# ODE layer inside the eigenvector block: matrix scaled ahead of V's scaling and the row statistics, powers copied at shorter distance

## What is computed

```
h = jnp.einsum('bnd,ed->bne', x, fc_in_w) + fc_in_b
alph = jax.nn.sigmoid(alpha_train)[:, None]
w_eff = w * jnp.clip(d, 0.0, 1.0) @ w.T
for _ in range(8):
    ax = jnp.einsum('nm,bmd->bnd', adj_mx, h)
    h = h + (1/8) * (alph * 0.5 * (ax - h) + h @ w_eff - h + x0)
```

## Time and profile before

| | us |
|---|---|
| median of 3 runs | 6786.41 (6783.37 to 6788.06) |
| profiled execution, device time | 6792.14 |
| its span, first to last instruction | 6790.4 |
| busy in the span: PE, DVE, ACT | 5355.4, 4564.6, 2311.9 |
| the block of the change, about | 4084 to 4673 |
| V's scaling in it | 4093.00 |
| recurrence in it | 4116 to 4551 |
| loop over batches on PE in it | 4192.09 to 4596.4 |

### The profile page before, as it was taken

How to read it: one execution, slowest core, us unless ns; L and a number is a source line. 1 busy time by engine, 2 the same in 40 slices (tenths; PEclk the granted TensorE clock), 3 DMA queues, 4 the chain that set the end, 5 groups by cost and what they waited for, 6 DMA issues and landing times. The chain is left out here.

```text
span 6790.4 us, 109815 instructions
## 1 busy us (share of the span) xinstructions
PE 5355.4 (79%) x33047; PEld 3803.4 (56%) x33047; DVE 4564.6 (67%) x27007; ACT 2311.9 (34%) x7369; POOL 93.6 (1%) x128
## 2 busy tenths in 40 slices
PE   4666788888877769969899976993546699776999
PEld 4555566666666534446566653662333477554676
DVE  7888888888888853379999997775562333424333
ACT  1222222222222235449599881110110233201333
POOL 0000000000000000000000000000000000000000
PEclk9999999999999999969999987996778799876999
DMA  1000000000000000010000000000000000000000
GB/s 46 2 2 2 2 3 5 3 4 4 4 4 3 4 21 13 7 54 6 6 4 6 4 3 8 1 1 0 25 28 0 13 0 0 9 0 13 0 0 25
DMA packets 27823, 56.57 MB, mean 8 GB/s; under 512 B 6186, under 2 KB 16835, under 8 KB 25539
## 3 DMA queue, kind: packets, MB, share of 16 engines
q1 hardware_dynamic: 27330, 50.79, 2.2%
HBM read 38.20 MB, written 12.58 MB: 7 GB/s over the span
## 5 line engine op out<-in xcount | busy, mean ns | idle before, releaser
L2007 DVE SCALAR_TENSOR_TENSOR f_ACC<-f_yp,f_CG,f_ACC 128x128 f32<-128x128 f32 x1024 | 288.4, 344 | 461.6 <-DVEq L2005 461.6
L1952 PEld LDWEIGHTS f_yp<-f_W,f_hs 128*128 128x128 f32 x4096 | 490.0, 192 | 92.6 <-issue 91.8
L1886 PE MATMUL f_hp<-f_rows,f_W 128*128 128x512 f32 x1024 | 531.5, 602 | 5.1 <-ACT U L1896 3.0
L1054 ACT ACTIVATE e_XD<-e_X,e_scal 128x60 f32<-128x60 f32 x2048 | 527.5, 333 | 17.5 <-DVEq L918 15.7
L710 PE MATMUL h_small<-h_part,ones 128*128 128x2 f32 x1024 | 300.6, 363 | 294.3 <-DVE h_jd L579 198.4
L1983 ACT ACTIVATE f_hs<-f_hp,f_b 128x512 f32<-128x512 f32 x512 | 347.7, 685 | 539.7 <-ACTq L1982 539.7
L655 ACT ACTIVATE h_VW<-h_v,h_s 128x8 f32<-128x8 f32 (+3 forms) x512 | 154.8, 302 | 1082.6 <-DVE h_s L417 1082.6
L1942 PE MATMUL f_hp<-f_XT,f_W 128*128 x1024 | 484.4, 601 | 33.0 <-PEq L2236 33.0
L703 PEld LDWEIGHTS h_ax<-h_XM,h_parts 128*128 128x128 bf16 x11520 | 480.8, 114 | 40.9 <-issue 40.9
L1952 PE MATMUL f_yp<-f_W,f_hs 128*128 128x128 f32 x4096 | 493.5, 275 | 0.0
L710 PEld LDWEIGHTS h_small<-h_part,ones 128*128 128x128 f32 x1024 | 256.6, 311 | 415.0 <-DVE h_jd L579 287.6
(11 more groups left out here) (716 smaller groups left out, 11363.2 us busy)
## 6 DMA issues: line engine op xcount, KB each, us to landing
f_S<-in_f_W SPq DMA_DIRECT2D x64, 128.0 KB, 2.3
X<-in_x SPq DMA_DIRECT2D x1, 4096.0 KB, 16.3
held<-g0e_HL SPq DMA_DIRECT2D x16, 256.0 KB, 2.0
g_HL<-held SPq DMA_DIRECT2D x16, 256.0 KB, 2.8
f_W<-in_f_W SPq DMA_DIRECT2D x2, 2048.0 KB
spill<-f_xts SPq DMA_DIRECT2D x16, 256.0 KB, 2.0
f_rows<-spill SPq DMA_DIRECT2D x16, 256.0 KB, 2.7
f_W<-in_f_W SPq DMA_DIRECT2D x4, 1024.0 KB
```

The lines of the kernel that those rows point to most:

```text
L1054: ins = nc.scalar.activation(XD[b][:, k, h, :], X[:, :], ACT.Identity, bias=scal[b][:, k, 2 * h:2 * h + 1])
L1886: nc.tensor.matmul(self.hp[s % 3][:, :], self.W1[:, e, j * P:(j + 1) * P], self.rows[:, g % 2, :], start=True, stop=True).then_inc(self.h_ ...
L1952: ins = nc.tensor.matmul(yp[:, u % 2, k, :], hs[:, u % 2, c, k * P:(k + 1) * P], W2[:, u * UC + c, :], start=(c == 0), stop=(c == UC - 1))
L2007: ins = V_.scalar_tensor_tensor(ACC[:, k, :], yp[:, u % 2, k, :], CG[:, k * E + e:k * E + e + 1], ACC[:, k, :], ALU.mult, ALU.add)
```

## The change

`start` loses the `bn_stats` and the row statistics, and is called ahead of V's scaling instead of behind the small instructions that follow it. It ends with the copy of the identity to R[0]. The rest is a new method `statistics`, called where `start` was: first R[1] (which was in `vector`, L2897), then the 64 `bn_stats`, the statistics, and the copy to R[2] between the variance and the wait for the square root. The other two copies of powers stay in `vector`, which loses the 4 ticks ahead of the first copy and the 17 behind it, and puts 12 and 6 ticks instead of 17 and 17 behind the second and third. On ScalarE the square root is moved from ahead of the copies of L1T to behind the copies of L2T.

```diff
@@ recurrence's block, VectorE @@
                     dve.wait_ge(ch, done.next())
+                    side.start(dve)
                     V_.tensor_tensor(V[:, :, :], V[:, :, :], G[:, :].unsqueeze(1).broadcast_to([P, NB, N]), ALU.mult).then_inc(ch, 1)
...
-                    side.start(dve)
+                    side.statistics(dve)
                     side.begin(dve)
@@ class Ode @@
     def start(self, dve):
...
-        for t in range(T):
-            V_.bn_stats(self.st[:, t, :], self.X[:, t, :]).then_inc(ch, 1)
-            done.next()
         dve.wait_ge(self.loaded, 16 * len(self.pairs))
...
+        V_.tensor_copy(self.R[:, 0, :], C.ident[:, :]).then_inc(ch, 1)
+        done.next()
+
+    def statistics(self, dve):
+
...
+        dve.wait_ge(self.r_out, 1)
+        V_.tensor_scalar(self.R[:, 1, :], self.PR[:, 0:D], 1.0 / self.STEPS, None, ALU.mult).then_inc(self.r_in, 1)
+        for t in range(T):
+            V_.bn_stats(self.st[:, t, :], self.X[:, t, :]).then_inc(ch, 1)
+            done.next()
+        dve.wait_ge(ch, done.n)
...
         V_.tensor_tensor(v, a, b, ALU.add).then_inc(self.var_in, 1)
-        V_.tensor_copy(self.R[:, 0, :], C.ident[:, :]).then_inc(ch, 1)
-        done.next()
+        self.wider_power(dve, 0)
         dve.wait_ge(self.sd_out, 1)
...
+    def wider_power(self, dve, k):
+
+        lo, hi = ((2, 3), (3, 5), (5, 9))[k]
+        dve.wait_ge(self.r_out, k + 2)
+        self.nc.vector.tensor_copy(self.R[:, lo:hi, :].rearrange("p m d -> p (m d)"), self.PR[:, 0:(hi - lo) * D]).then_inc(self.r_in, 1)
...
-        dve.wait_ge(self.r_out, 1)
-        V_.tensor_scalar(R[:, 1, :], PR[:, 0:D], 1.0 / STEPS, None, ALU.mult).then_inc(self.r_in, 1)
         for n in range(NB):
             ins = self.row_block(0, n)
             if n == NB - 1:
                 ins.then_inc(self.x_full, 1)
             yield 2
-        yield 4
-        for k, (lo, hi) in enumerate(((2, 3), (3, 5), (5, 9))):
-            dve.wait_ge(self.r_out, k + 2)
-            V_.tensor_copy(R[:, lo:hi, :].rearrange("p m d -> p (m d)"), PR[:, 0:(hi - lo) * D]).then_inc(self.r_in, 1)
-            yield 17
+        for k in (1, 2):
+            self.wider_power(dve, k)
+            yield 12 if k == 1 else 6
...
@@ scalar @@
         nc.scalar.activation(self.al[:, :], self.al[:, :], ACT.Sigmoid).then_inc(self.sg, 1)
-        act.wait_ge(self.var_in, 1)
-        nc.scalar.activation(self.sd[:, :], self.v[:, :], ACT.Sqrt).then_inc(self.sd_out, 1)
         for out, made, full in ((self.L1T, self.l1t_out, self.l1t_in), (self.L2T, self.l2t_out, self.l2t_in),
                                 (self.L3T, self.l3t_out, self.l3t_in), (self.L3, self.l3_out, self.l3_in),
                                 (self.L6T, self.l6t_out, self.l6t_in)):
+            if out is self.L3T:
+                act.wait_ge(self.var_in, 1)
+                nc.scalar.activation(self.sd[:, :], self.v[:, :], ACT.Sqrt).then_inc(self.sd_out, 1)
```

More of the change, by code:

```diff
@@ L2837, in start @@
         V_, ch, done, C = self.nc.vector, self.ch, self.done, self.C
-        st, a, b, v, mean, rstd = (t[:, :] for t in (self.st[:, :, 0], self.a, self.b, self.v, self.mean, self.rstd))
-        for t in range(T):
-            V_.bn_stats(self.st[:, t, :], self.X[:, t, :]).then_inc(ch, 1)
-            done.next()
         dve.wait_ge(self.loaded, 16 * len(self.pairs))
@@ L2855, in start @@
             V_.scalar_tensor_tensor(blk, C.ident[:, :], self.a78[:, n:n + 1], blk, ALU.mult, ALU.add).then_inc(self.l1_made, 1)
+        V_.tensor_copy(self.R[:, 0, :], C.ident[:, :]).then_inc(ch, 1)
+        done.next()
+    def statistics(self, dve):
+        V_, ch, done = self.nc.vector, self.ch, self.done
+        a, b, v, mean, rstd = (t[:, :] for t in (self.a, self.b, self.v, self.mean, self.rstd))
+        dve.wait_ge(self.r_out, 1)
[4 more added lines that the diff above has]
+        dve.wait_ge(ch, done.n)
         me, mo, qe, qo = self.st[:, :, 1], self.st[:, :, 4], self.st[:, :, 2], self.st[:, :, 5]
```

## The result

| | before | after |
|---|---|---|
| median of 20 runs each, us | 6786.90 (6778.36 to 6795.39) | 6796.63 (6792.15 to 6805.64) |
| profiled execution, device time | 6792.14 | 6796.60 |
| its span | 6790.4 | 6794.9 |
| block of the change: first load of `e_Z` to first matmul of the next stage | 589.25 | 593.13 |
| back transformation, the stage behind it | 119.39 | 124.39 |

A forecast was written before the change was run, and what follows sets the result against it. DVE was taken to end the block: 24.1 us of steps moved behind its last wait, less 20.55 of PE's advance and about 0.2, gave +3.3 on the median 6786.41, so 6789.7 us, range 6780 to 6797.

The forecast's parts named there:

- The clock of PE: PE's start times from the transposes to the loop: moved earlier, by 15.19 us at first and 20.55 at the loop.
- The second half of the bias row: PE's second L3062, behind DVE's Gm: starts at 4142.6 in the old trace's times, 20.55 us earlier.
- The last wait: DVE's 14th wait for PE's row blocks (`ty_out`): passed at about 4510.9 in the old trace's times.
- The waits of DVE: Second way to the sum: DVE's work is unchanged, 3.0 us of new wait and 0.3 of small gaps give +3.3.
- The wait for the root: DVE ahead of its reciprocal, for ACT's square root behind L2T's copies and a table load: 3.2 us instead of 0.19.
- The add of HS in the 15th turn: DVE in the tail, reached about when PE's product is ready: extra wait taken as 0, at most 0.3 us.
- the 37 steps: Recurrence steps moved from ahead of the loop to behind DVE's last wait for PE: 24.1 us more there.
- Rival 1: At the block's end, PE's advance is paid out in full: 20.55 us earlier, 6765.8 us; chance 0.04.
- Rival 2: PE's L2T at half clock, with the root behind it: 13.9 us more, 6803.6 us; chance 0.03.
- Rival 3: PE's clock stays up ahead of the loop: DVE's longest wait some 7.7 us shorter, 6782.0 us; chance 0.07.
- the change lies in one stretch, so the difference goes to the median: From block to whole kernel: the block's +3.3 us is added to the median 6786.41, giving 6789.7.
- the likeliest case: Whole kernel, the forecast +3.3 us with its bounds: 6786.4 to 6791.8 us, chance 0.85.

The follow-up runs named there:

- ticks-back run: Changed kernel with the recurrence's steps put back between the copies (yield 29 and 26 instead of 12 and 6): 6789.02 us, 1.0006 of the kernel before.
- once more: Changed kernel run again with no edit: 6795.25 us, 1.0016 of the kernel before.
- only a delay: Kernel before plus one idle DVE reciprocal of an unused tile behind V's scaling: 6791.86 us, 1.0010 of the kernel before.
- root ahead of L2T's copies: Changed kernel with ACT's square root moved to behind the copies of L1T: 6796.81 us, 1.0018 of the kernel before.
- shorter filler: Changed kernel plus 56 unread matmul calls behind PE's loop, 48.23 us long: 6795.18 us, 1.0010 of the kernel before.
- filler past the end: Changed kernel plus 230 unread matmul calls behind PE's loop, 197.58 us, past the end of DVE's work: 6894.29 us, 1.0154 of the kernel before.
- before, turns of 32: Kernel before with TURN, the recurrence steps DVE does between row blocks, 32 instead of 29: 6775.61 us, 0.9984 of the kernel before.
- changed, turns of 32: Changed kernel with TURN, the recurrence steps DVE does between row blocks, 32 instead of 29: 6768.25 us, 0.9972 of the kernel before.
- two us more: Changed kernel with one DVE instruction behind the recurrence (Z times Z) done twice, 2.3 us more work: 6794.53 us, 1.0013 of the kernel before.
- changed, turns of 34: Changed kernel with TURN, the recurrence steps DVE does between row blocks, set to 34: 6758.74 us, 0.9964 of the kernel before.

## Why the prediction was right, and which term was missing

**The clock of PE.** Each step of the prediction, made in the times of the trace before, stands in the trace after once 5.47 is taken off. Transposes: 4091.60 forecast, 4091.60 measured. L2T: 4095.93 and 4095.95. The second half of the bias row: 4137.13 and 4137.29. The loop: 4166.03 and 4166.06. The last wait: 4505.43 and 4505.48. The next stage was to begin at about 4671.5 and did at 4672.08. PE's idle time ahead of L3068 (the old L3056) was 1.43, forecast 1.9. Ticks counted at 0.65 us held to 0.3 us over this stretch of 75 us. That the loop came out to 0.03 is partly luck: the first row block was 0.32 late (4114.90, forecast 4114.58), and the 12 ticks behind the copy of R[3:5] took 7.83 us (4120.51 to 4128.34) instead of 8.0.

**The waits of DVE.** The wait for the root was 3.49, forecast 3.2. L2T took 14.34 us instead of 13.90: the granted clock was 0.65 in its first 1.05 us, where it had been 1.00 before. The prediction had kept 1.8 for this between its bounds and taken none. The root began 1.30 us behind the start of the table load, about as an activation in the trace before (1.42). The Trainium skill (ScalarE: Activation LUTs, What ACT_TABLE_LOAD costs) gives about 2.66 us for a switch with its drain; this trace has 4112.23 - 4110.93 = 1.30 and doesn't agree. The add of HS in the 15th turn waited 0.44, where 0 was taken and 0.3 the bound. The block's sum is (3.49 - 0.19) + 0.44 + 0.15 of a small gap ahead of L1234 = 3.89, and the block got longer by 3.88, with DVE's work in it the same (453.06 us before, 452.99 after). By PE's clock it is 24.37 more behind the last wait (142.23 to 166.60) less 20.49 of advance at it, where the prediction had 24.1 - 0.2 and 20.55. The prediction had 3.3: **this part was right, 0.3 short at the root and 0.4 at HS**.

**No gain from PE's advance.** The loop came 20.56 us earlier, the 37 steps stand behind the last wait, and the ticks-back run shows the two as equal: 592.65 against 593.13. Rival 1 falls. The 3.3 us of delay alone gave +3.33 of block, so the price of standing still at that place is shown by itself too. Taking the wait away gave back only 0.63, since other waits took its place. Rival 2 (L2T at half clock) cost 0.44 of its 13.9. Rival 3 didn't come: after 4.84 us of idling the loop's first product (L3095, the old L3083) is 15.72 us long, as in the earlier trace rows, and DVE's longest wait 12.8.

**The term that was missing.** The prediction's step "the change lies in one stretch, so the difference goes to the median" is the one that failed. It took every stage behind the block at the length that it had, without a word on them, and the back transformation was 5.0 longer. With it the sum is 3.9 + 5.0 = 8.9, and the median moved by 9.7. (The profiles have 1.09 more behind that stage, 9.97 in all from the block's start on; the second trace of the changed kernel has 9.87.) The trace of before had the hint: a granted clock of 0.68, 0.87 and 0.98 in that stage, that is a clock on the move through it, and a forecast that shifts such a stage by 3.3 us (and what lies ahead of it on PE by 20) owes a bound for its length. A bound could have been estimated from the rows: the second stretch of 40 us has PE busy for 26.80 at 0.87, and at the 0.68 of the first these would be 26.80 x 0.87/0.68 = 34.3, 7.5 us more. That the range held the result was luck: 6796.63 lies 0.4 us inside its end of 6797, the likeliest case ended at 6791.8, at 6794.8 with the 3 us by which the runs spread, and the last step to 6797 isn't worked out in it.

What the runs exclude as the cause of the 5 us: chance (124.39 twice), a later end alone (119.11), the length of PE's idle time between 53.6 and 101.7 us (124.38), the edit to the order of the instructions ahead of the recurrence (118.35 with the ticks back and all else in place). What they show: the same program with 2.3 us more work in front has 118.96, with the clock higher in the second stretch. The early loop isn't the cause by itself, as that run and the one with 34 ticks (119.05) have it as well. So the mechanism is shown as far as this: the 5 us are PE's clock in that stage. That it hangs on where the stage falls in time is what the runs point to: the three kernels in which the stage starts some 481.5 us behind the loop's start took 118.35 to 119.39, the four at 506.0 or 478.7 us took 124.34 to 124.39. Another layout of the code is a rival that no run was made for; against it speaks that the filler and the turns of 32 change the code and leave the stage at 124.4.

**What stays open.** What decides where the clock changes isn't settled: over all kernels the stage took 115.78 to 125.16, and neither its distance from the loop nor the block's length puts them in order: at the same 474.0 us behind the loop the kernel before with turns of 32 has 115.78 and the changed one with turns of 34 has 119.05. In timed runs the part outside the block can't be resolved:

| | median's move less the block's, us | stage in the profile, us |
|---|---|---|
| changed kernel | +5.8 | +5.0 |
| once more | +5.8 | +5.0 |
| only a delay | +2.9 | -0.3 |
| root ahead of L2T's copies | +8.0 | +5.8 |
| ticks back | 0.0 | -1.0 |
| shorter filler | +3.4 | +5.0 |
| filler past the end | +4.0 | +2.2 |
| before, turns of 32 | -4.6 | -3.6 |
| changed, turns of 32 | +4.1 | +5.0 |
| two us more | +4.2 | -0.4 |
| changed, turns of 34 | +3.0 | -0.3 |

Each has some 4 to 10 us of uncertainty. So the timed runs agree with the profile's 5 us in the changed kernel and don't show them by themselves. The stage with 16 batches of attention was 323.76 before, 322.86 with the delay, and 325.7 to 326.5 in all others, the changed kernel with 325.76 among them: 2 us that no run explains.

## What to carry to other kernels

In a block that ends with one in-order engine, an edit is worth what it does to that engine's waits and work, and to nothing else: here PE came 20.56 us earlier and the end 3.88 later, as the sum of one new wait and two small ones had it. Work moved out from under a neighbour's time is no gain until the freed slots are filled again: the early loop was worth nothing with turns of 29 ticks and 16 us with 32. When TensorE's granted clock is on the move in the stage behind the edit, put a bound on that stage too before calling the rest unchanged, and compare variants by several shifts of its start rather than by one.

## What the hardware did that had not been expected

Where the clock changes is repeated from one execution of a program to the next: the back transformation took 124.39 us in both traces of the changed kernel, though its block began 4.1 us later in the second, and the granted clock in slices of 5 us was the same to 0.01. The program with a filler ahead of the stage has 124.38. Another, 2.3 us shifted, has another pattern and 118.96. By the traces the time of one variant can therefore be 5 us better or worse than its work deserves, and repeating that variant alone won't show it.

A matmul call on f32 data of 128 x 512 is two instructions of 0.43 us: 112 for 56 calls, 460 for 230, 48.23 and 197.58 us. Both fillers were meant half as long as they became.
